# Four-layer network on one core: the first feed-forward layer's weights are loaded during the attention before it

## The chip, the cores and the metric

The kernel is one program on one core of a Trainium2 chip. It has five engines with a queue of their own (TensorE or PE, VectorE or DVE, ScalarE or ACT, GpSimd or POOL, SyncE or SP); SP issues nearly all DMAs. The metric is the device time of one execution in microseconds (us); lower is better. The time before the change is the median of three runs, 3949.11 us (3946.87 to 3950.89).

## What is computed

Four layers run one after the other on 2048 tokens of width 256 (2 sequences of 1024). Each layer normalises its input once and adds the outputs of an attention part and of a feed-forward part, both computed from that same normalised input. The first layer is the one that matters here:

```python
xn = _layernorm(x, axis=-1)
x = x + _L0_attn_ref(xn, w_q, w_kv, w_dense) + _L0_ffn_ref(xn, SU_ug, SU_dp, Wscale_ug, Wscale_dp, W_up, W_gate, W_down)

# attention: 16 heads of 128 in 4 groups, causal softmax
q, k, v = xn @ w_q, xn @ w_k, xn @ w_v
out = (softmax(mask(q @ k.T * scale)) @ v) @ w_dense

# feed-forward, 1024 wide; fwht is a normalised Walsh-Hadamard transform
x = fwht(x * SU_ug) / SCALE
x_up = x @ W_up.T * (Wscale_ug[:INTER] * SCALE)
x_gate = x @ W_gate.T * (Wscale_ug[INTER:] * SCALE)
x = jax.nn.silu(x_gate) * x_up
x = fwht(x * SU_dp) / SCALE
x = x @ W_down.T * (Wscale_dp * SCALE)
```

The kernel applies the transforms to the weights instead of the tokens: before the first token is multiplied, W_up, W_gate and W_down are multiplied by a Hadamard matrix and split into a high and a low part.

## The kernel before

A `Stage` is a scope: it allocates buffers and semaphores and gives them back at its end. Inside it, an `nc.Block` holds one instruction stream for each engine. All engines meet at a barrier at the end of a block, so nothing of the next block, its DMAs included, is issued before the last engine of this one is done. Within a block only semaphores order the engines; each engine takes its own instructions strictly in the order written, and so does SP with its DMAs.

`program` (L2735) runs the first layer as a normalisation, a split of the tokens into high and low parts, then `l0_attn` (L209), a block that clears semaphores, and `l0_ffn` (L550).

`l0_heads` (L274) loops over 16 heads. Each head has 16 blocks of 128 queries (`U`), and for these 20 software-pipelined steps s. In step s, PE makes the scores of block s (L355), transposes the probabilities of block s-2 (L369), multiplies the context of block s-4 by the dense weights (`dense`, L391) and weighs the values of block s-3 (L382). ACT in step s copies the context of block s-4 (L521), copies transposed probabilities (L514) and computes the exponentials of block s (L528). In step 4 (`SPLIT_AT`), between the copies and the exponential, ACT rounds the next head's query weights: `split_weights(h+1)` (L490 to L492), which waits for their load.

SP's stream in this block is short. It loads `wq` and `wd` of head 0 (L318, L319) and then loops over the other heads: the load of `wq` for head h waits for `wlo_ready` (L322, the previous head's query weights are used up), the load of `wd` for head h waits for `dense_done` of the previous head (L324). `wq` has one buffer.

`l0_ffn` begins with a small stage of its own, `l0w`: SP issues nine loads (L581 to L589: the Hadamard matrix `had`, `raw` for W_up and W_gate, `rawd` for W_down, and five small columns). DVE waits for all nine (`loaded`, L626) and negates `had` (L627); PE waits for that and multiplies `raw` and `rawd` by `had` (L600, L606); ACT and DVE split the products; DVE then does the rest of the transform of W_down (L645 to L654). Only after this block does the loop over tokens begin (L661 on).

```python
                def split_weights(h):
                    act.wait_ge(wq_loaded, h * 16 + 16)
                    wait(act, q_made, h * NJ)
                    act.activation(wq_hi[:, :, :], wq[:, :, :], ACT.Copy).then_inc(whi_ready, 1)
```

Of the kernel before, what the change touches and what calls it, by code (L numbers as in the profile page):

```python
# [16 lines left out]
P = 128  # L17
# [3 lines left out]
DC = D // P  # L21
# [6 lines left out]
class Stage:  # L28
# [5 lines left out]
    def __init__(self, nc, name):  # L34
        self.nc, self.name, self.ctx = nc, name, ExitStack()
# [35 lines left out]
def rows(w):  # L71

    return w.rearrange("(c p) n -> p c n", p=P)
# [134 lines left out]

def l0_attn(nc, k, a):  # L209
    with Stage(nc, "l0a") as st:  # L210
        KT = st.sb("KT", [P, L0_GROUPS, T])
        V = st.sb("V", [P, TT, L0_GROUPS * L0_HD])
        l0_kv(nc, k, a, KT, V)
        l0_heads(nc, k, a, KT, V)

# [57 lines left out]

def l0_heads(nc, k, a, KT, V):  # L274

# [7 lines left out]
    with Stage(nc, "l0h") as st:  # L283
# [22 lines left out]
        ctxT_ready, probs_scaled, vg_ready, copies = st.sem("ctxT_ready"), st.sem("probs_scaled"), st.sem("vg_ready"), st.sem("copies")  # L306
        dense_done, added = st.sem("dense_done"), st.sem("added")

        SPLIT_AT = 4
# [4 lines left out]
        with nc.Block() as block:  # L314

            @block.sync
            def _(sp):
                sp.dma_start(wq[:, :, :], rows(a["L0_attn_w_q"])[:, :, 0:P]).then_inc(wq_loaded, 16)  # L318
                sp.dma_start(wd[:, :], a["L0_attn_w_dense"][0:P, :]).then_inc(wd_loaded, 16)  # L319
                with sp.Fori(1, L0_HEADS) as h:  # L320
                    sp.wait_ge(wlo_ready, h)
                    sp.dma_start(wq[:, :, :], rows(a["L0_attn_w_q"])[:, :, ds(h * P, P)]).then_inc(wq_loaded, 16)  # L322
                    sp.wait_ge(dense_done, h * U)
                    sp.dma_start(wd[:, :], a["L0_attn_w_dense"][ds(h * P, P), :]).then_inc(wd_loaded, 16)  # L324

                sp.wait_ge(wlo_ready, L0_HEADS)
                sp.dma_start(wq[:, :, :], rows(a["L0_attn_w_q"])[:, :, 0:P]).then_inc(wq_loaded, 16)

            @block.tensor
# [219 lines left out]

def l0_ffn(nc, k, a):  # L550


    with Stage(nc, "l0f") as st:
# [3 lines left out]
        wd_hi, wd_lo = st.sb("wd_hi", [P, L0_FC, D], F32R), st.sb("wd_lo", [P, L0_FC, D], F32R)  # L557
        su = st.sb("su", [P, DC])
        sd = st.sb("sd", [P, L0_FC])
        su_n = st.sb("su_n", [P, DC])  # L560
        sd_n = st.sb("sd_n", [P, L0_FC])
        s_up = st.sb("s_up", [P, L0_FC])
        s_gate = st.sb("s_gate", [P, L0_FC])
        s_down = st.sb("s_down", [P, DC])
        with Stage(nc, "l0w") as s2:
            had = s2.sb("had", [P, 2, P])
            raw = s2.sb("raw", [P, 2, DC, L0_INTER])
            rawd = s2.sb("rawd", [P, L0_FC, D])
            bf0 = s2.sb("bf0", [P, L0_FC, D])
# [3 lines left out]
            acc = [s2.ps(f"acc{i}") for i in range(8)]  # L573
            loaded, made, kept, had_ready, flown = s2.sem("loaded"), s2.sem("made"), s2.sem("kept"), s2.sem("had_ready"), s2.sem("flown")
            NL = 9

            with nc.Block() as block:

                @block.sync
                def _(sp):  # L580
                    sp.dma_start(had[:, 0, :], a["c_had"]).then_inc(loaded, 16)  # L581
                    sp.dma_start(su[:, :], a["L0_ffn_SU_ug_cols"]).then_inc(loaded, 16)
                    sp.dma_start(raw[:, 0, :, :], rows(a["L0_ffn_W_upT"])).then_inc(loaded, 16)
                    sp.dma_start(raw[:, 1, :, :], rows(a["L0_ffn_W_gateT"])).then_inc(loaded, 16)
                    sp.dma_start(rawd[:, :, :], rows(a["L0_ffn_W_downT"])).then_inc(loaded, 16)
                    sp.dma_start(sd[:, :], a["L0_ffn_SU_dp_cols"]).then_inc(loaded, 16)
                    sp.dma_start(s_up[:, :], a["L0_ffn_Wscale_ug_cols"][:, 0:L0_FC]).then_inc(loaded, 16)
                    sp.dma_start(s_gate[:, :], a["L0_ffn_Wscale_ug_cols"][:, L0_FC:2 * L0_FC]).then_inc(loaded, 16)
                    sp.dma_start(s_down[:, :], a["L0_ffn_Wscale_dp_cols"]).then_inc(loaded, 16)  # L589

# [34 lines left out]
                def _(dve):  # L625
                    dve.wait_ge(loaded, 16 * NL)  # L626
                    dve.tensor_scalar(had[:, 1, :], had[:, 0, :], -1.0, None, ALU.mult).then_inc(had_ready, 1)  # L627
# [2103 lines left out]
SPLIT_LAYERS = (0, 1)  # L2731
LAYERS = [(l0_attn, l0_ffn), (l1_attn, l1_ffn), (l2_attn, l2_ffn), (l3_attn, l3_ffn)]


def program(nc, a):  # L2735


    with ExitStack() as ctx:
# [12 lines left out]
        for i, (attn, ffn) in enumerate(LAYERS):  # L2751
            norm_stage(nc, k, f"n{i}", k.XT, k.XN)
            with Stage(nc, f"x{i}") as sx:
                if i in SPLIT_LAYERS:
                    k.XH, k.XL = sx.sb("XH", [P, DC, T], F32R), sx.sb("XL", [P, DC, T], F32R)
                    split_stage(nc, f"s{i}", k.XN, k.XH, k.XL)
                attn(nc, k, a)
                clear_semaphores(nc)
                ffn(nc, k, a)
                clear_semaphores(nc)  # L2760

# [48 lines left out]
```

## Time and profile before

| | |
|---|---|
| median of three runs | 3949.11 us (3946.87 to 3950.89) |
| span of the profiled execution | 3953.8 us |
| PE busy | 3518.6 us, 89% of the span |
| DVE, ACT, POOL busy | 60%, 39%, 35% of the span |
| DMA engines busy | about 15% of 16 engines' span |
| first layer's attention (`l0_heads`) | from 99 to 1043 us of the span |
| first layer's weight loads and transforms (`l0w`) | from 1043 to 1089 us |

For the profiled execution the profile gives its span and no time beside it. The span runs from the first to the last instruction and is 4.7 us, or 0.1%, longer than the median of the timed runs. In the trace, PEclk is the TensorE clock that was granted in a stretch, as a share of full speed: 1.00 is 2.4 GHz and 0.50 is 1.2 GHz. "Idle before <-X" in brackets is the time for which the engine waited before the instruction and what ended the wait. SPq stands for SP's queue of DMA issues; an issue is short, and the data land later ("us to landing" counts from the issue).

### The profile page before, as it was taken

The numbers are of one execution on the slowest core, as the hardware profiler recorded it, in microseconds if no ns is written. First come the engines' busy times: TensorE is split into PE (matmuls) and PEld (weight loads), VectorE is DVE, ScalarE is ACT, GpSimd is POOL, SyncE is SP. The second block draws the span as 40 slices with busy tenths as digits, with TensorE's granted clock in tenths as the row PEclk, the third lists the DMA queues.
The fourth block names the chain that finished last, engine by engine and source line by source line (L and its number), as shares of the span: only waits on it lengthen the run. The fifth ranks groups of instructions, "written<-read, shape, count | busy, mean of one in ns | idle before, by whom it ended". The sixth has DMA issues, their size and how long they took to land. (4 is left out here: it accounts for less than half of the span.)

```text
span 3953.8 us, 65993 instructions
## 1 busy us (share of the span) xinstructions
PE 3518.6 (89%) x21608; PEld 2645.3 (67%) x21608; DVE 2363.0 (60%) x4783; ACT 1546.2 (39%) x2820; POOL 1385.1 (35%) x1085
## 2 busy tenths in 40 slices
PE   6899999999796999999995779998699988999576
PEld 4777777777574888888872445554388847886354
DVE  3555555655423566666654879885477756776454
ACT  2444444444333444444432236664333333333121
POOL 1333333332133666666652200000133352335144
PEclk8999999999898999999997879999799998999755
DMA  0000000000001000000000412221233304331144
GB/s 33 7 5 3 5 5 3 5 5 5 33 0 43 13 18 17 17 17 17 17 5 22 171 65 82 80 83 39 65 93 103 105 10 107 98 96 48 60 108 96
DMA packets 115990, 178.66 MB, mean 45 GB/s; under 512 B 22288, under 2 KB 65040, under 8 KB 115600
## 3 DMA queue, kind: packets, MB, share of 16 engines
q1 hardware_dynamic: 109776, 169.38, 13.7%
q0 software_dynamic: 6144, 8.39, 1.3%
q8 instruction: 38, 0.62, 0.1%
q14 instruction: 32, 0.26, 0.0%
HBM read 151.51 MB, written 25.95 MB: 45 GB/s over the span
## 5 line engine op out<-in xcount | busy, mean ns | idle before, releaser
L424 POOL TENSOR_TENSOR l0h_probs<-l0h_probs,l0h_inv 128x128 f32<-128x128 f32 (+7 forms) x256 | 292.7, 1146 | 585.4 <-DVE l0h_inv L459 585.4
L1775 DVE TENSOR_REDUCE l2h_half<-l2h_s 128x1 f32<-128x512 f32 x512 | 337.3, 685 | 48.0 <-PE l2h_s L1677 47.0
L355 PE MATMUL l0h_sc<-l0a_KT,l0h_QT 128*128 x768 | 296.7, 499 | 29.8 <-ACT l0h_probs L528 28.3
L1762 ACT ACTIVATE l2h_PT<-l2h_s 128x1024 f32<-128x1024 f32 x256 | 248.3, 1022 | 162.6 <-PE l2h_s L1687 162.5
L382 PE MATMUL l0h_cx<-l0h_PT,l0h_VG 128*128 128x128 f32 x2304 | 300.7, 276 | 0.0
L528 ACT ACTIVATE l0h_probs<-l0h_sc,l0h_negtop 128x128 f32<-128x128 f32 (+7 forms) x256 | 189.6, 741 | 245.0 <-DVE l0h_negtop L454 244.6
L382 PEld LDWEIGHTS l0h_cx<-l0h_PT,l0h_VG 128*128 128x128 f32 x2304 | 278.0, 192 | 1.1
L159 POOL TENSOR_TENSOR XN<-XN,n_rstd 128x512 f32<-128x512 f32 x32 | 39.8, 1266 | 595.8 <-DVE n_rstd L140 595.8
L1677 PE MATMUL l2h_s<-l2h_K,l2h_Q 128*128 128x512 f32 x512 | 218.5, 466 | 23.2 <-DMA l2h_K<-l_split 21.0
L452 DVE TENSOR_REDUCE l0h_top<-l0h_sc 128x1 f32<-128x128 f32 (+7 forms) x256 | 193.9, 758 | 8.8
L355 PEld LDWEIGHTS l0h_sc<-l0a_KT,l0h_QT 128*128 128x128 f32 x768 | 125.7, 192 | 106.3 <-issue 63.6
L391 PE MATMUL l0h_outp<-l0h_ctxT,l0h_wd 128*128 128x128 f32 x1024 | 163.8, 283 | 24.8 <-ACT l0h_ctxT L521 11.7
L369 PEld LDWEIGHTS l0h_tp<-ident,l0h_probs 128*128 128x128 f32 x1152 | 138.6, 141 | 64.1 <-issue 39.5
L1677 PEld LDWEIGHTS l2h_s<-l2h_K,l2h_Q 128*128 128x128 f32 x512 | 99.2, 195 | 113.4 <-DVE l2h_half L1775 74.7
L369 PE MATMUL l0h_tp<-ident,l0h_probs 128*128 128x128 f32 x1152 | 168.7, 273 | 0.0
L470 DVE COPY l0h_PT<-l0h_tp 128x256 f32<-128x256 f32 (+2 forms) x192 | 98.6, 514 | 114.2 <-PE l0h_tp L369 112.4
L2189 POOL TENSOR_TENSOR l3p_w_lo<-l3p_w,l3p_w_hi 128x1024 fp32r<-128x1024 f32 x34 | 80.1, 2356 | 241.1 <-ACT l3p_w_hi L2145 241.1
L391 PEld LDWEIGHTS l0h_outp<-l0h_ctxT,l0h_wd 128*128 128x128 f32 x1024 | 134.2, 191 | 44.7 <-ACT l0h_ctxT L521 31.2
L514 ACT ACTIVATE l0h_PT<-l0h_tp 128x512 f32<-128x512 f32 (+1 forms) x192 | 100.8, 525 | 159.8 <-PE l0h_tp L369 159.3
L2221 DVE TENSOR_TENSOR_SCAN l3p_table<-l3p_decb,l3p_eye 128x512 f32<-128x512 f32 x128 | 149.6, 1210 | 22.8 <-DMA l3p_blk<-c_l_block 17.3
L1687 PE MATMUL l2h_s<-l2h_Q,l2h_K 128*128 128x512 f32 x512 | 161.7, 399 | 0.0
L2179 POOL TENSOR_TENSOR l3a_Y<-l3p_skip,l3p_sz 128x512 f32 (+1 forms) x64 | 81.6, 1276 | 208.9 <-DVE l3p_skip L2212 208.9
(408 smaller groups left out, 8954.9 us busy)
## 6 DMA issues: line engine op xcount, KB each, us to landing
l3p_decb<-l_decays SPq DMA_DIRECT2D x128, 256.0 KB, 4.2
l3p_w<-L_w SPq DMA_DIRECT2D x34, 512.0 KB, 3.7
l2h_Q<-l_split SPq DMA_DIRECT2D x64, 256.0 KB
l2h_K<-l_split SPq DMA_DIRECT2D x64, 256.0 KB
l3p_prow<-l_decays SPq DMA_DIRECT2D x128, 128.0 KB, 2.9
l_split<-l2q_hi SPq DMA_DIRECT2D x16, 512.0 KB, 4.1
l_split<-l2q_lo SPq DMA_DIRECT2D x16, 512.0 KB, 3.8
mx_wgu<-L_ffn_w_gate_up SPq DMA_DIRECT2D x32, 256.0 KB
```

The source lines that it names most:

```text
L355: mm = pe.matmul(sc[u % 2][:, lo:lo + n], QT[:, u * P:(u + 1) * P], KT[:, ds(g, 1), b * S + lo:b * S + lo + n], start=True, stop=True)
L369: mm = pe.transpose(tp[n % 2][:, (kb - q) * P:(kb - q + 1) * P], probs[:, u % 4, kb * P:(kb + 1) * P], k.ident[:, :])
L382: mm = pe.matmul(cx[:, 0:P], VG[:, b * NQ + kb, :], PT[:, u % 2, kb, :], start=(kb == 0), stop=(kb == t))
L391: mm = pe.matmul(outp[:, c * P:(c + 1) * P], wd[:, c * P:(c + 1) * P], ctxT[:, u % 2, :], start=True, stop=True)
L424: pool.tensor_tensor(p, p, inv[:, u % 4:u % 4 + 1].to_broadcast([P, keys(u)]), ALU.mult).then_inc(probs_scaled, 1)
L452: dve.reduce_max(top[:, u % 2:u % 2 + 1], sc[u % 2][:, 0:keys(u)], AX_X).then_inc(top_ready, 1)
L528: act.activation(probs[:, u % 4, 0:keys(u)], sc[u % 2][:, 0:keys(u)], ACT.Exp, bias=negtop[:, u % 2:u % 2 + 1], scale=L0_SCALE, accum_out= ...
L1677: pe.matmul(bank(slot_of(i))[:, :], Q1[:, b, t * P:(t + 1) * P], K1[:, b, z * BANK:(z + 1) * BANK], start=True, stop=True).then_inc(s1_mad ...
L1687: mm = pe.matmul(s2[kb % 2][:, z * BANK:(z + 1) * BANK], K2[:, b, kb * P:(kb + 1) * P], Q2[:, b, z * BANK:(z + 1) * BANK], start=True, sto ...
L1762: act.activation(PT[:, b, kb, :], s2[kb % 2][:, :], ACT.Exp, scale=L2_SCALE).then_inc(exped, 1)
L1775: dve.reduce_max(half[:, b, t, z:z + 1], bank(slot_of(i))[:, :], AX_X).then_inc(s1_read, 1)
L2221: dve.tensor_tensor_scan(table[:, i, :], decb[:, o, i, :], eye4[:, :], 0.0, ALU.mult, ALU.add).then_inc(tables, 1)
```

## The change

The nine buffers that the feed-forward part's loads fill move into a class `L0Weights`, in a stage `l0r` that is open over both the attention and the feed-forward part, so that they lie beside the attention's buffers instead of in their place. The nine loads move from the feed-forward part's first block into SP's stream in `l0_heads`: behind the loads of head 0's weights and a new wait for the first `dense_done`, and ahead of the loop over the other heads. At the end of its stream SP waits until all nine have landed. The stage `l0w` has no SP stream any more, and DVE's wait for `loaded` is gone. All other instructions are the same.

```diff
@@ -206,12 +206,35 @@
 L0_SCALE = L0_HD ** -0.5
-def l0_attn(nc, k, a):
+class L0Weights:
+
+
+    def __init__(self, st):
+        self.had = st.sb("had", [P, 2, P])
+        self.raw = st.sb("raw", [P, 2, DC, L0_INTER])
+        self.rawd = st.sb("rawd", [P, L0_FC, D])
+        self.su = st.sb("su", [P, DC])
+        self.sd = st.sb("sd", [P, L0_FC])
+        self.s_up = st.sb("s_up", [P, L0_FC])
+        self.s_gate = st.sb("s_gate", [P, L0_FC])
+        self.s_down = st.sb("s_down", [P, DC])
+
+
+def l0_layer(nc, k, a):
+    with Stage(nc, "l0r") as st:
+        raws = L0Weights(st)
+        l0_attn(nc, k, a, raws)
+        clear_semaphores(nc)
+        l0_ffn(nc, k, a, raws)
+        clear_semaphores(nc)
+
+
+def l0_attn(nc, k, a, raws):
     with Stage(nc, "l0a") as st:
         KT = st.sb("KT", [P, L0_GROUPS, T])
         V = st.sb("V", [P, TT, L0_GROUPS * L0_HD])
         l0_kv(nc, k, a, KT, V)
-        l0_heads(nc, k, a, KT, V)
+        l0_heads(nc, k, a, KT, V, raws)
 def l0_kv(nc, k, a, KT, V):
@@ -305,6 +328,8 @@
         turned, pt_act, pt_dve, pv_done = st.sem("turned"), st.sem("pt_act"), st.sem("pt_dve"), st.sem("pv_done")
         ctxT_ready, probs_scaled, vg_ready, copies = st.sem("ctxT_ready"), st.sem("probs_scaled"), st.sem("vg_ready"), st.sem("copies")
         dense_done, added = st.sem("dense_done"), st.sem("added")
+        raw_loaded = st.sem("raw_loaded")
+        NL = 9
         SPLIT_AT = 4
@@ -317,6 +342,16 @@
             def _(sp):
                 sp.dma_start(wq[:, :, :], rows(a["L0_attn_w_q"])[:, :, 0:P]).then_inc(wq_loaded, 16)
                 sp.dma_start(wd[:, :], a["L0_attn_w_dense"][0:P, :]).then_inc(wd_loaded, 16)
+                sp.wait_ge(dense_done, 1)
+                sp.dma_start(raws.had[:, 0, :], a["c_had"]).then_inc(raw_loaded, 16)
+                sp.dma_start(raws.su[:, :], a["L0_ffn_SU_ug_cols"]).then_inc(raw_loaded, 16)
+                sp.dma_start(raws.raw[:, 0, :, :], rows(a["L0_ffn_W_upT"])).then_inc(raw_loaded, 16)
+                sp.dma_start(raws.raw[:, 1, :, :], rows(a["L0_ffn_W_gateT"])).then_inc(raw_loaded, 16)
+                sp.dma_start(raws.rawd[:, :, :], rows(a["L0_ffn_W_downT"])).then_inc(raw_loaded, 16)
+                sp.dma_start(raws.sd[:, :], a["L0_ffn_SU_dp_cols"]).then_inc(raw_loaded, 16)
+                sp.dma_start(raws.s_up[:, :], a["L0_ffn_Wscale_ug_cols"][:, 0:L0_FC]).then_inc(raw_loaded, 16)
+                sp.dma_start(raws.s_gate[:, :], a["L0_ffn_Wscale_ug_cols"][:, L0_FC:2 * L0_FC]).then_inc(raw_loaded, 16)
+                sp.dma_start(raws.s_down[:, :], a["L0_ffn_Wscale_dp_cols"]).then_inc(raw_loaded, 16)
                 with sp.Fori(1, L0_HEADS) as h:
                     sp.wait_ge(wlo_ready, h)
                     sp.dma_start(wq[:, :, :], rows(a["L0_attn_w_q"])[:, :, ds(h * P, P)]).then_inc(wq_loaded, 16)
@@ -325,6 +360,7 @@
                 sp.wait_ge(wlo_ready, L0_HEADS)
                 sp.dma_start(wq[:, :, :], rows(a["L0_attn_w_q"])[:, :, 0:P]).then_inc(wq_loaded, 16)
+                sp.wait_ge(raw_loaded, 16 * NL)
             @block.tensor
             def _(pe):
@@ -547,7 +583,7 @@
 L0_FC = L0_INTER // P
-def l0_ffn(nc, k, a):
+def l0_ffn(nc, k, a, raws):
     with Stage(nc, "l0f") as st:
@@ -555,38 +591,19 @@
         wu_hi, wu_lo = st.sb("wu_hi", [P, DC, L0_INTER], F32R), st.sb("wu_lo", [P, DC, L0_INTER], F32R)
         wg_hi, wg_lo = st.sb("wg_hi", [P, DC, L0_INTER], F32R), st.sb("wg_lo", [P, DC, L0_INTER], F32R)
         wd_hi, wd_lo = st.sb("wd_hi", [P, L0_FC, D], F32R), st.sb("wd_lo", [P, L0_FC, D], F32R)
-        su = st.sb("su", [P, DC])
-        sd = st.sb("sd", [P, L0_FC])
         su_n = st.sb("su_n", [P, DC])
         sd_n = st.sb("sd_n", [P, L0_FC])
-        s_up = st.sb("s_up", [P, L0_FC])
-        s_gate = st.sb("s_gate", [P, L0_FC])
-        s_down = st.sb("s_down", [P, DC])
+        had, raw, rawd, su, sd = raws.had, raws.raw, raws.rawd, raws.su, raws.sd
+        s_up, s_gate, s_down = raws.s_up, raws.s_gate, raws.s_down
         with Stage(nc, "l0w") as s2:
-            had = s2.sb("had", [P, 2, P])
-            raw = s2.sb("raw", [P, 2, DC, L0_INTER])
-            rawd = s2.sb("rawd", [P, L0_FC, D])
             bf0 = s2.sb("bf0", [P, L0_FC, D])
             bf1 = s2.sb("bf1", [P, L0_FC, D])
             wdn = s2.sb("wdn", [P, L0_FC, D])
             low, wd_ready = s2.sem("low"), s2.sem("wd_ready")
             acc = [s2.ps(f"acc{i}") for i in range(8)]
-            loaded, made, kept, had_ready, flown = s2.sem("loaded"), s2.sem("made"), s2.sem("kept"), s2.sem("had_ready"), s2.sem("flown")
-            NL = 9
+            made, kept, had_ready, flown = s2.sem("made"), s2.sem("kept"), s2.sem("had_ready"), s2.sem("flown")
             with nc.Block() as block:
-
-                @block.sync
-                def _(sp):
-                    sp.dma_start(had[:, 0, :], a["c_had"]).then_inc(loaded, 16)
...
-                    sp.dma_start(s_down[:, :], a["L0_ffn_Wscale_dp_cols"]).then_inc(loaded, 16)
                 @block.tensor
                 def _(pe):
@@ -623,7 +640,6 @@
                 @block.vector
                 def _(dve):
-                    dve.wait_ge(loaded, 16 * NL)
                     dve.tensor_scalar(had[:, 1, :], had[:, 0, :], -1.0, None, ALU.mult).then_inc(had_ready, 1)
                     dve.tensor_scalar(su_n[:, :], su[:, :], D ** -0.5, None, ALU.mult).then_inc(had_ready, 1)
                     dve.tensor_scalar(sd_n[:, :], sd[:, :], L0_INTER ** -0.5, None, ALU.mult).then_inc(had_ready, 1)
@@ -2729,7 +2745,7 @@
 SPLIT_LAYERS = (0, 1)
-LAYERS = [(l0_attn, l0_ffn), (l1_attn, l1_ffn), (l2_attn, l2_ffn), (l3_attn, l3_ffn)]
+LAYERS = [(None, None), (l1_attn, l1_ffn), (l2_attn, l2_ffn), (l3_attn, l3_ffn)]
 def program(nc, a):
@@ -2754,10 +2770,13 @@
                 if i in SPLIT_LAYERS:
                     k.XH, k.XL = sx.sb("XH", [P, DC, T], F32R), sx.sb("XL", [P, DC, T], F32R)
                     split_stage(nc, f"s{i}", k.XN, k.XH, k.XL)
-                attn(nc, k, a)
-                clear_semaphores(nc)
-                ffn(nc, k, a)
-                clear_semaphores(nc)
+                if i == 0:
+                    l0_layer(nc, k, a)
+                else:
+                    attn(nc, k, a)
+                    clear_semaphores(nc)
+                    ffn(nc, k, a)
+                    clear_semaphores(nc)
```

**Where the instructions stand.** The first place is SP, from the loads of head 0's weights on. Names beginning with l0h are the attention's buffers, l0w and l0f the feed-forward part's, l0r the new stage's. Before, the loop's load of `wq` (L322) stood two rows behind head 0's, and the nine loads stood in the next block, of which this shows only the start of the list:

```order
L318 DMA l0h_wq<-L_attn_w_q 128x2x128
L319 DMA l0h_wd<-L_attn_w_dense 128x256
L320 UNCONDITIONAL_BRANCH
L322 ISA [waits l0h_wlo_ready]
L322 DMA l0h_wq<-L_attn_w_q 128x2x128
L323 REGISTER_ALU
L324 ISA [waits l0h_dense_done]
L324 DMA l0h_wd<-L_attn_w_dense 128x256
L320 REGISTER_ALU
```

Now, from the row behind head 0's two loads on:

```order
L346 DMA l0r_had<-c_had 128x128 [waits l0h_dense_done]
L347 DMA l0r_su<-L_ffn_SU_ug_cols 128x2
L348 DMA l0r_raw<-L_ffn_W_upT 128x2x1024
L349 DMA l0r_raw<-L_ffn_W_gateT 128x2x1024
L350 DMA l0r_rawd<-L_ffn_W_downT 128x8x256
L351 DMA l0r_sd<-L_ffn_SU_dp_cols 128x8
L352 DMA l0r_s_up<-L_ffn_Wscale_ug_cols 128x8
L353 DMA l0r_s_gate<-L_ffn_Wscale_ug_cols 128x8
L354 DMA l0r_s_down<-L_ffn_Wscale_dp_cols 128x2
L355 UNCONDITIONAL_BRANCH
L357 ISA [waits l0h_wlo_ready]
L357 DMA l0h_wq<-L_attn_w_q 128x2x128
```

The nine loads and a wait for `dense_done` now stand between the load of `wd` for head 0 and the load of `wq` for head 1.

The second place is DVE, at the start of the feed-forward part's weight stage. Before:

```order
L624 UNCONDITIONAL_BRANCH [waits barrier_Pool_Activation_PE_DVE_SP_release]
L627 TENSOR_SCALAR l0w_had<-l0w_had 128x128 [waits l0w_loaded]
L628 TENSOR_SCALAR l0f_su_n<-l0f_su 128x2
L629 TENSOR_SCALAR l0f_sd_n<-l0f_sd 128x8
L636 SCALAR_TENSOR_TENSOR l0f_wu_lo<-l0w_acc,l0f_su_n,l0f_wu_hi 128x512 [waits l0w_had_ready,l0w_kept]
```

Now:

```order
L641 UNCONDITIONAL_BRANCH [waits barrier_Pool_Activation_PE_DVE_SP_release]
L643 TENSOR_SCALAR l0r_had<-l0r_had 128x128
L644 TENSOR_SCALAR l0f_su_n<-l0r_su 128x2
L645 TENSOR_SCALAR l0f_sd_n<-l0r_sd 128x8
L652 SCALAR_TENSOR_TENSOR l0f_wu_lo<-l0w_acc,l0f_su_n,l0f_wu_hi 128x512 [waits l0w_had_ready,l0w_kept]
```

The wait for `l0w_loaded` is gone; the order is the same.

The third place is ACT, in step 4 of a head, in the changed kernel; before, the same rows stand there, with L528 as L492 and L564 as L528:

```order
L550 ACTIVATE l0h_PT<-l0h_tp 128x384 [waits l0h_pv_done,l0h_turned]
L526 ISA
L80 REGISTER_ALU [waits l0h_wq_loaded]
L528 ACTIVATE l0h_wq_hi<-l0h_wq 128x256 [waits l0h_q_made]
L560 REGISTER_ALU
L564 ACTIVATE l0h_probs,l0h_total<-l0h_sc,l0h_negtop 128x640 [waits l0h_turned,l0h_negtop_ready]
```

Nothing moved on ACT: its wait for `wq_loaded` stands ahead of the exponential of the fifth block (L564).

## Rows read from the trace of the kernel before

**Rows 1.** The page's first line.

```profile
span 3953.8 us, 65993 instructions
```

**Rows 2.** Stretches: length, busy us (instructions) of each engine, PEclk, DMA share, GB/s.

```profile
99.00:1043.00 944.00, 884.32 (x5656) 707.45 (x5656) 527.50 (x1473) 421.49 (x1061) 312.41 (x281) 0.99 0.02 5
1043.00:1088.70 45.70, 19.45 (x40) 8.31 (x40) 18.06 (x29) 10.19 (x17) 0.00 (x0) 0.76 0.21 71
```

**Rows 3.** Timeline at the border of attention and feed-forward: start us, us, engine.

```profile
1041.28 0.71 PE L391 MATMUL l0h_outp<-l0h_ctxT,l0h_wd 128*128 128x128 f32 x4 [0.37 <-ACT l0h_ctxT L521]
1042.02 0.42 DVE L475 TENSOR_TENSOR XT<-XT,l0h_outp 128x256 f32<-128x256 f32 x1 [2.44 <-PE l0h_outp L391]
1043.24 0.34 SPq L581 DMA_DIRECT2D l0w_had<-c_had  x1
...
1045.10 0.47 SPq L585 DMA_DIRECT2D l0w_rawd<-L_ffn_W_downT  x1
1045.61 3.25 SPq L586 DMA_DIRECT2D l0f_sd<-L_ffn_SU_dp_cols  x1
...
1049.91 0.43 SPq L589 DMA_DIRECT2D l0f_s_down<-L_ffn_Wscale_dp_cols  x1
1055.87 0.23 DVE L627 TENSOR_SCALAR l0w_had<-l0w_had 128x128 f32<-128x128 f32 x1 [13.42 <-DMA l0f_s_down<-L_ffn_Wscale_dp_cols]
...
1056.15 16.02 PE L600 MATMUL l0w_acc<-l0w_raw,l0w_had 128*128 128x512 f32 x32 [14.16 <-DVE l0w_had L627]
```

**Rows 4.** DMA issues from 1040 to 1060 us: KB each, us to landing.

```profile
l0w_raw<-L_ffn_W_upT SPq DMA_DIRECT2D x1, 1024.0 KB, 5.4
...
l0w_rawd<-L_ffn_W_downT SPq DMA_DIRECT2D x1, 1024.0 KB, 9.5
...
l0f_sd<-L_ffn_SU_dp_cols SPq DMA_DIRECT2D x1, 4.0 KB, 9.2
...
l0f_s_down<-L_ffn_Wscale_dp_cols SPq DMA_DIRECT2D x1, 1.0 KB, 5.9
```

**Rows 5.** Stretches about the weight transforms, columns as in rows 2.

```profile
1042.00:1044.00 2.00, 0.00 (x0) 0.00 (x0) 0.42 (x1) 0.00 (x0) 0.00 (x0) 1.00 0.00 0
...
1046.00:1048.00 2.00, 0.00 (x0) 0.00 (x0) 0.00 (x0) 0.00 (x0) 0.00 (x0) 0.65 1.01 389
...
1056.00:1060.00 4.00, 3.85 (x5) 1.78 (x6) 0.24 (x3) 0.00 (x0) 0.00 (x0) 0.50 0.00 0
...
1062.00:1076.00 14.00, 13.60 (x32) 5.70 (x30) 5.26 (x7) 6.87 (x11) 0.00 (x0) 1.00 0.00 0
```

**Rows 6.** Timeline of head 0 about its step 4, columns as in rows 3.

```profile
103.14 0.39 SPq L322 DMA_DIRECT2D l0h_wq<-L_attn_w_q  x1
...
119.60 0.68 PE L391 MATMUL l0h_outp<-l0h_ctxT,l0h_wd 128*128 128x128 f32 x4
...
120.04 0.41 ACT L492 ACTIVATE l0h_wq_hi<-l0h_wq 128x256 fp32r<-128x256 f32 x1
...
120.84 0.79 ACT L528 ACTIVATE l0h_probs<-l0h_sc,l0h_negtop 128x640 f32<-128x640 f32 x1 [0.39 <-DVE l0h_negtop L454]
...
122.29 0.61 PE L391 MATMUL l0h_outp<-l0h_ctxT,l0h_wd 128*128 128x128 f32 x4
```

**Rows 7.** Timeline at the end of head 0, columns as in rows 3.

```profile
169.11 0.71 PE L391 MATMUL l0h_outp<-l0h_ctxT,l0h_wd 128*128 128x128 f32 x4 [0.37 <-ACT l0h_ctxT L521]
...
169.99 0.35 SPq L324 DMA_DIRECT2D l0h_wd<-L_attn_w_dense  x1
```

**Rows 8.** DMA issues from 99 to 121 us, columns as in rows 4.

```profile
l0h_wq<-L_attn_w_q SPq DMA_DIRECT2D x2, 128.0 KB, 2.2
```

**Rows 9.** Stretches early in the attention, columns as in rows 2.

```profile
101.00:102.00 1.00, 0.00 (x0) 0.00 (x0) 0.00 (x0) 0.26 (x1) 0.00 (x0) 0.55 0.64 179
...
103.00:107.00 4.00, 3.99 (x9) 3.14 (x10) 0.00 (x0) 0.60 (x1) 1.93 (x2) 0.50 0.11 33
...
121.00:131.00 10.00, 10.00 (x66) 7.86 (x65) 7.41 (x19) 4.93 (x12) 5.08 (x4) 1.00 0.01 2
```

More of the change, by code:

```diff
@@ L271, in _, with l0_heads @@
                     dve.tensor_copy(target(n), acc[n % 8][:, :]).then_inc(kept_dve, 1)
-def l0_heads(nc, k, a, KT, V):
+def l0_heads(nc, k, a, KT, V, raws):
     U = B * NQ
@@ L573, in l0_ffn @@
             acc = [s2.ps(f"acc{i}") for i in range(8)]
-            loaded, made, kept, had_ready, flown = s2.sem("loaded"), s2.sem("made"), s2.sem("kept"), s2.sem("had_ready"), s2.sem("flown")
-            NL = 9
+            made, kept, had_ready, flown = s2.sem("made"), s2.sem("kept"), s2.sem("had_ready"), s2.sem("flown")
             with nc.Block() as block:
-                @block.sync
-                def _(sp):
-                    sp.dma_start(had[:, 0, :], a["c_had"]).then_inc(loaded, 16)
[L582 to L588, printed above, removed]
-                    sp.dma_start(s_down[:, :], a["L0_ffn_Wscale_dp_cols"]).then_inc(loaded, 16)
                 @block.tensor
```

## The prediction

> **What bounds the kernel now.** I read the stretches by stage first. The attention of the first layer takes 944 us with PE busy for 884 of them; the stretch behind it, in which the feed-forward weights are loaded and transformed, takes 45.7 us with PE busy for 19.5 [rows 2]. So PE bounds the attention, and the stretch behind it is a chain of waits. The timeline shows the chain. The last matmul of the attention ends at 1041.99 (1041.28 + 0.71), the last DVE instruction at 1042.44; SP issues the first of nine loads at 1043.24; DVE negates the Hadamard matrix only at 1055.87, released by the ninth load; PE begins at 1056.15 [rows 3]. Look at the bracket of the DVE row: 13.42 us idle, ended by a DMA. No engine has work in these 12.6 us, so they lie wholly on the path. The landing times tell why it lasts that long: three loads of 1 MB keep all 16 DMA engines busy (share 1.01, 389 GB/s [rows 5]), and a 4 KB load issued behind them lands 9.2 us after its issue [rows 4].
>
> The second place to read is where the loads go. In head 0 the load of `wq` for head 1 is issued at 103.14 and used by ACT at 120.04: it has 17 us and needs 2.2 [rows 6, 8]. In the changed order it stands behind a wait for the first `dense_done` and behind the nine loads, and ACT's wait for it stands ahead of an exponential that everything else in the head hangs on. That is where I look for the price.
>
> **Part 1, the loads leave the feed-forward part: a gain of 12.6 us.** DVE's first instruction now waits only for the barrier. The barrier let SP go at 1043.24 [rows 3]; I let DVE start at the same time, 12.6 us earlier. All loads have landed some 900 us before. Bounds: 12.3 (a barrier that frees DVE 0.3 later) to 12.7.
>
> **Part 2, the clock in the transforms: a gain of 2.2 us.** PE's granted clock is still 1.00 from 1042 to 1044, is falling from 1046 to 1048 (mean 0.65), and is at 0.50 when the transforms begin: from 1056 to 1060 PE needs 3.85 us for 5 matmul records, later 13.60 us for 32, or 0.43 each [rows 5]. Now PE is idle only from 1041.99 to about 1043.5, a time through which the clock stayed at 1.00 before. At full clock the 32 records take 13.6 us plus some 0.2 for the last to end, against 16.02 [rows 3, 5], so 2.2 us less. Everything up to the end of the transforms follows PE here. Bounds: 0 (the clock falls all the same) to 2.4.
>
> **Part 3, ACT waits in head 0: a loss of 13.0 us.** First, when SP goes on. At the end of head 0 the dense matmuls begin at 169.11 and SP's issue that waits for them comes at 169.99, 0.88 later [rows 7]. The first dense matmuls begin at 119.60 [rows 6], so SP issues its first moved load at about 120.5. The nine issues took 7.1 us before (1043.24 to 1049.91 + 0.43, one of them 3.25 us long [rows 3]), so `wq` is issued at about 127.6. The ninth load landed 12.6 us after the first issue (1049.91 + 5.9 = 1055.8 [rows 3, 4]), now at 133.1. `wq` is 128 KB behind it, 0.3 us at 389 GB/s, and lands at 133.4. ACT's rounding starts there in place of 120.04, 13.4 us late. Behind it on ACT is the exponential of block 4; it used to wait 0.39 us for DVE [rows 6] and will not any more, so it comes 13.0 us late. Behind that on ACT is the copy of context 1, for which PE's dense matmuls of 122.29 wait [rows 6]; PE, DVE and POOL have only what is already released, about 2 us of it. From 121 to 131 PE was busy for 10.00 of 10 us [rows 9], so there is no slack in which the head could catch up.
>
> Bounds: the lower is a `wq` that lands 2.2 us after its issue [rows 8], at 129.8, whatever is before it: a loss of 9.4. The upper is 14, if the transfers are a tenth slower than they were with every engine idle. I take the value behind the queue, because the nearest row is the 4 KB load that needed 9.2 us behind 3 MB [rows 4]. The page "DMA: Bandwidth & Descriptors" of the Trainium skill, section "Queues, rings and completion order", says that completion is "not FIFO per issuing engine". Taken by itself for `wq`, that would make this part 9.4 and the time 3945.9 us. The small load's 9.2 us in this trace speaks for the same page's other sentence, that each DMA engine takes up its ring in order.
>
> **Part 4, the clock in head 0: a loss of 2.2 us.** PE stands still from about 122.3 to 135. A pause of this length took the clock to 0.50 at the border [rows 5], and a shorter one at 101 us did too (mean 0.55 [rows 9]). On its return PE worked at 0.50 for at least 4 us, busy for 3.99 of them [rows 9]. Where PE is the bound, half of such a time is lost: 2.0 for 4 us, 2.5 for 5, and I take 2.2. Bounds: 0 (PE has no full work then) to 2.75 (5.5 us).
>
> **At nothing.** SP's wait at the end of the block costs nothing while the loads land 900 us earlier; if they did not, the barrier would wait for them. The load of `wd` for head 1 still waits for the end of head 0. The buffers' new addresses and the missing SP stream cost nothing that the trace shows. The layers behind are unchanged.
>
> **Sum.** -12.6 - 2.2 + 13.0 + 2.2 = +0.4 us. The profiled execution spans 3953.8 us [rows 1], 4.7 more than the median; I add the difference to the median, 3949.11 + 0.4 = 3949.5 us. The load has not left the path, it has moved from one border to one head. With the bounds of all parts together the difference runs from -5.7 (-12.7 - 2.4 + 9.4 + 0) to +4.5 (-12.3 + 0 + 14 + 2.75, rounded).
>
> **The rivals.** About 0.2% of the time, 7.9 us, is what a measurement of this kernel can tell from no change.
>
> *A, `wq` overtakes the large loads.* For it: 128 KB is little, and nothing orders the loads but the queue. Against it: the 9.2 us of 4 KB [rows 4]. Then part 3 is 9.4 and the time 3945.9 us. Chance 0.09.
>
> *B, the clock falls at the border all the same.* For it: the row of 101 us shows a fall within a short pause [rows 9]. Against it: 1.00 from 1042 to 1044 [rows 5]. Part 2 is 0, the time 3951.7 us. Chance 0.09.
>
> *C, faster: the heads take up the stall.* In the attention PE is idle for 60 of 944 us [rows 2]. If the engines behind ACT had work in store, or the stall used up waits that come anyway, parts 3 and 4 would vanish and 3934.3 us would be left. Against it: PE is at 10.00 of 10 us where the stall falls [rows 9], and each block needs its exponential. Chance 0.07.
>
> *D, slower: PE stays at the low clock in head 0.* After the stall PE works in a chain with ACT and DVE; if its pauses keep the clock at 0.50, half of each microsecond of its work is lost. It decides from about 19 us at the low clock: 9.5 in place of 2.2 makes the sum +7.7. If it lasts for the rest of head 0, some 49 us of PE work (120 to 169) become 98, and the time is 3996 us. Against it: after 103 us the clock was back at 1.00 by 121 [rows 9]. Chance 0.07.
>
> *E, the change does not do what it says*, in that something else still holds DVE at the border. The barrier's own time is in the 1043.24; nothing else stands ahead of L643. It would leave +15 us; I hold it within D's 0.07.
>
> **How the numbers follow.** The forecast has 0.68, A and B 0.09 each, C and D 0.07 each. A and B lie within 7.9 us, so: faster 0.07, same 0.86, slower 0.07. The range is 3943 to 3955 us: the sum of all bounds gives 3943.4 to 3953.6, and the three runs before spread over 4 us. C and D are left out.
>
> **What would show it.** In the changed kernel DVE negates the matrix about 0.8 us behind the attention's last DVE instruction; the transforms run at clock 1.00 from the start; ACT's second rounding in head 0 has an idle time of about 13 us ended by the load of `wq`; PE has a hole of about 12 us behind its scores of block 5, and the clock is at 0.50 for 4 to 5 us behind it. Head 1 begins about 15 us later than before. I am wrong if that hole is not there or is much shorter, if `wq` lands before `rawd`, or if any other stage differs by more than a microsecond or two.

## The result, and the profile after

| | before | after |
|---|---|---|
| median | 3950.76 us (3944.20 to 3958.32, 20 runs) | 3959.11 us (3949.59 to 3962.67, 20 runs) |
| span of the profiled execution | 3953.8 us | 3957.9 us |

The changed kernel is slower: ratio 1.0018, 95% interval 1.0011 to 1.0024, or 7.1 us (4.3 to 9.5) on 3951; the two medians lie 8.35 us apart, and this text goes by the ratio. The forecast was 3949.5 us and no change, within 3943 to 3955. It was built on 3949.11 us, the median of three runs; twenty give 3950.76, so 1.65 of the 9.6 us between forecast and measurement are the base.

Two words for what follows: the border is the time from the attention's last addition (DVE) to the negation of the Hadamard matrix (DVE), and the kv projection is the block ahead of the heads in which PE makes keys and values (`l0_kv`). The moved buffers are eight, not nine: two of the nine loads fill `raw`.

Head 0 of the changed kernel, timeline (start us, us, engine):

```profile
123.75 0.94 PE L427 MATMUL l0h_outp<-l0h_ctxT,l0h_wd 128*128 128x128 f32 x4
...
124.72 0.34 SPq L346 DMA_DIRECT2D l0r_had<-c_had  x1
...
127.08 2.81 SPq L351 DMA_DIRECT2D l0r_sd<-L_ffn_SU_dp_cols  x1
...
131.94 0.40 SPq L357 DMA_DIRECT2D l0h_wq<-L_attn_w_q  x1
137.76 0.42 ACT L528 ACTIVATE l0h_wq_hi<-l0h_wq 128x256 fp32r<-128x256 f32 x1 [13.27 <-DMA l0h_wq<-L_attn_w_q]
138.09 0.78 ACT L564 ACTIVATE l0h_probs<-l0h_sc,l0h_negtop 128x640 f32<-128x640 f32 x1
...
138.85 0.27 ACT L557 ACTIVATE l0h_ctxT<-l0h_cx 128x128 f32<-128x128 f32 x1
...
139.17 1.22 PE L427 MATMUL l0h_outp<-l0h_ctxT,l0h_wd 128*128 128x128 f32 x4 [12.31 <-ACT l0h_ctxT L557]
```

The wait that was foretold is there: ACT's second rounding sits idle for 13.27 us, ended by the load of `wq`, and PE has a hole of 12.31 us behind it. Set against [rows 6, 7]: SP's first moved load comes 0.97 us after the dense matmuls begin (0.88 in the forecast), `wq` is issued 7.2 us after that (7.1 in the forecast), and the rounding follows 13.0 us after the first issue (12.9). The landing times, columns as in [rows 4]:

```profile
l0r_rawd<-L_ffn_W_downT SPq DMA_DIRECT2D x1, 1024.0 KB, 9.9
l0h_wq<-L_attn_w_q SPq DMA_DIRECT2D x1, 128.0 KB, 5.7
...
l0r_sd<-L_ffn_SU_dp_cols SPq DMA_DIRECT2D x1, 4.0 KB, 9.6
```

`wq`, last in the queue, lands at 131.94 + 5.7 = 137.6, and `rawd`, which was issued at 126.57, at 126.57 + 9.9 = 136.5: `wq` did not overtake the large loads. The 128 KB that took 2.2 us alone [rows 8] took 5.7.

The border, timeline; before it was [rows 3]:

```profile
1062.66 0.71 PE L427 MATMUL l0h_outp<-l0h_ctxT,l0h_wd 128*128 128x128 f32 x4 [0.37 <-ACT l0h_ctxT L557]
1063.41 0.42 DVE L511 TENSOR_TENSOR XT<-XT,l0h_outp 128x256 f32<-128x256 f32 x1 [2.44 <-PE l0h_outp L427]
1064.68 0.23 DVE L643 TENSOR_SCALAR l0r_had<-l0r_had 128x128 f32<-128x128 f32 x1 [0.85 <-PEq L60]
```

From the last addition to the negation there are 1.27 us where there were 13.84. The first 32 records of the transforms, PE's timeline by itself:

```profile
1064.96 14.00 PE L617 MATMUL l0w_acc<-l0r_raw,l0r_had 128*128 128x512 f32 x32 [1.59 <-DVE l0r_had L643]
```

14.00 us in place of 16.02. The clock, stretches with columns as in [rows 2]:

```profile
139.00:145.00 6.00, 5.83 (x17) 4.08 (x18) 2.98 (x8) 1.39 (x4) 3.40 (x3) 0.51 0.00 0
145.00:151.00 6.00, 6.00 (x45) 5.00 (x44) 4.46 (x10) 3.11 (x6) 1.68 (x1) 1.00 0.00 0
...
1064.00:1066.00 2.00, 1.04 (x3) 0.56 (x4) 0.47 (x3) 0.00 (x0) 0.00 (x0) 1.00 0.01 4
```

PE is at full clock at the border (1064 to 1066). In head 0 it is at 0.51 for the 6 us behind the hole and at 1.00 after it. So each foretold step is there, in about its size. Something else is in the trace, and it begins before SP has issued anything new: in the kv projection, 50 us ahead of the moved loads. PE there fills one bank of results with 6 matmuls after another, and DVE copies every second bank, so that 12 matmuls lie between two copies. The timeline of before, then of after:

```profile
74.05 0.69 DVE L271 COPY l0a_KT<-l0kv_acc 128x512 f32<-128x512 f32 x1 [2.03 <-PE l0kv_acc L199]
76.77 0.69 DVE L271 COPY l0a_KT<-l0kv_acc 128x512 f32<-128x512 f32 x1 [2.03 <-PE l0kv_acc L199]
```

```profile
73.58 0.69 DVE L294 COPY l0a_KT<-l0kv_acc 128x512 f32<-128x512 f32 x1 [2.11 <-PE l0kv_acc L199]
76.38 0.69 DVE L294 COPY l0a_KT<-l0kv_acc 128x512 f32<-128x512 f32 x1 [2.11 <-PE l0kv_acc L199]
```

Twelve matmuls take 2.72 us before and 2.80 after, 0.227 and 0.233 us each. Those are matmuls of the keys. For the values, which follow, the view by tile gives the duration of one (ns, min/median/max), before and after:

```profile
L199 PE MATMUL l0kv_acc<-l0kv_w_hi,x_XH x32: 389/389/389, 76.6 to 97.6; 128*128 128x512 f32 x32
```

```profile
L199 PE MATMUL l0kv_acc<-l0kv_w_hi,x_XH x32: 391/397/400, 79.0 to 100.8; 128*128 128x512 f32 x32
```

They are the same instructions on the same data; of the two operands that PE reads, the tokens (`XH`, `XL`) lie where they lay, and the weights (`l0kv_w_hi`, `l0kv_w_lo`) have moved.

I divided each trace at fixed instructions. "To layer 1" runs from the load of the kv weights to layer 1's first load; "loop" is from the first gate matmul to the last addition. Head 15 and layer 1's normalisation have no column, so the columns do not add up to "to layer 1". The rows below after are kernels of the next section. Times in us:

| kernel | kv projection | head 0 | heads 1 to 14 | border | weight stage | loop | to layer 1 |
|---|---|---|---|---|---|---|---|
| before | 55.13 | 59.11 | 814.04 | 13.84 | 32.86 | 139.88 | 1219.78 |
| after | 57.09 | 75.90 | 815.49 | 1.27 | 30.82 | 141.29 | 1225.67 |
| e5_top | 55.26 | 73.57 | 814.41 | 1.27 | 30.82 | 139.77 | 1220.20 |
| e7_stall_alone | 55.33 | 73.70 | 814.82 | 13.77 | 33.82 | 138.72 | 1234.20 |
| e3_wq_first | 56.77 | 60.45 | 815.38 | 1.27 | 32.42 | 141.34 | 1211.33 |
| e6_top_wq_first | 55.34 | 59.12 | 814.30 | 1.27 | 30.81 | 138.75 | 1203.70 |
| e8_wq_between | 55.43 | 60.95 | 814.57 | 1.27 | 32.51 | 140.14 | 1209.70 |

After is 5.9 us behind before at layer 1, while its columns add up to 7.0. The other 1.1 us came back in layer 1's normalisation, between the loop's last addition and layer 1's first load: there PE's clock fell 18.6 us behind the last addition in the kernel before and 23.5 us behind it in the changed one. These stretches begin 18.6 us behind it, before and after:

```profile
1248.00:1252.80 4.80, 2.38 (x3) 0.33 (x1) 3.05 (x2) 0.69 (x1) 2.48 (x2) 0.50 0.00 0
```

```profile
1256.20:1261.00 4.80, 1.23 (x3) 0.19 (x1) 4.18 (x2) 0.69 (x1) 2.48 (x2) 1.00 0.00 0
```

The early fall is in before, e4, e5 and e8 to e11, the late one in after, e1, e2, e3, e6 and e7, so it goes with no one edit; it moves the time to layer 1 by 0.8 to 1.3 us. What follows layer 1's first load is unchanged code and takes 2689.7 us before and 2686.7 after; over all kernels here it took 2679 to 2690, with nothing that goes with the edit. That scatter is why the two spans (4.1 us apart) do not say the same as the medians.

### The profile page after: what moved, and what is told of

Same layout as the page of the kernel before. It is cut to its first block and busy times, and to the rows that moved or that the text cites. A ratio compares the mean times of both kernels' runs of the same rounds, so it can differ in the third digit from the quotient of the medians.

```text
span 3957.9 us, 65994 instructions
## 1 busy us (share of the span) xinstructions
PE 3521.8 (89%) x21608; PEld 2645.4 (67%) x21608; DVE 2363.8 (60%) x4783; ACT 1548.0 (39%) x2820; POOL 1374.1 (35%) x1085
## 5 line engine op out<-in xcount | busy, mean ns | idle before, releaser
L564 ACT ACTIVATE l0h_probs<-l0h_sc,l0h_negtop 128x128 f32<-128x128 f32 (+7 forms) x256 | 189.8, 741 | 244.1 <-DVE l0h_negtop L490 243.7
```

What stands on the lines that cost most here:

```text
L564: act.activation(probs[:, u % 4, 0:keys(u)], sc[u % 2][:, 0:keys(u)], ACT.Exp, bias=negtop[:, u % 2:u % 2 + 1], scale=L0_SCALE, accum_out= ...
```

## The experiments

There are two theories. A: the surplus over the forecast comes from the addresses to which the eight buffers, allocated first, push all others, and the sum of the forecast is right. B: it comes from the loads, the longer scope or a worse stall.

**The changed kernel, padded.** In e1, 32 unused bytes per partition lie behind the moved buffers:

```diff
         self.s_down = st.sb("s_down", [P, DC])
+        self.pad = st.sb("pad", [P, 8])
```

> The changed kernel with one spare column block of 32 bytes per partition behind the moved buffers, so that every buffer of the first layer starts 32 bytes later. Theory of the addresses (a 512-column matmul is slower when its two operands start in different 32-byte halves of a 64-byte line): the spacing of the key and value projection's matmuls falls from 0.234 us back to 0.227, its stage from 57.1 to 55.5 us, the gate and up projections' spacing too, and the time is 3 to 6 us below the changed kernel's, so about 0 to 4 us above the kernel before. Rival (the slower spacing is the chip's or the run's): spacing stays at 0.234 and the time at about 7 us above the kernel before.

Measured 3950.77 us, ratio 0.9999 (0.9991 to 1.0008). Thirty-two unused bytes took the loss away; layer 1 is reached 5.0 us sooner than in the changed kernel (1220.63), of which 1.1 is a clock that rose earlier in the loop, as in e6 below. Gate and up matmuls came to 0.229 us, but the kv projection stayed at 0.233: its expected fall to 0.227 did not come. So the 64-byte form of the theory is wrong, and which distance matters is taken up below.

**The kernel before, padded.** e2 is the reverse, 32 bytes ahead of the first layer's buffers and nothing else:

```diff
+                with Stage(nc, f"pad{i}") as sp_:
+                    if i == 0:
+                        sp_.sb("pad", [P, 8])
                     attn(nc, k, a)
```

> The kernel before with 32 bytes per partition ahead of the first layer's buffers, nothing else. Theory of the addresses: the spacing of the projections' matmuls rises from 0.227 to 0.234 us, the key and value stage takes 1.3 us more, the 16 heads together 1.5 to 2.6 more, gate and up 2.6 more, down no faster: 4 to 6 us above the kernel before. Rival: no difference in spacing or time.

Measured 3954.81 us, ratio 1.0012 (1.0002 to 1.0021). By tile:

```profile
L199 PE MATMUL l0kv_acc<-l0kv_w_hi,x_XH x32: 393/396/400, 78.9 to 100.6; 128*128 128x512 f32 x32
```

The matmuls are slow as in the changed kernel, with no load moved. "To layer 1" is 1225.33 us, 5.6 over before.

**The change with all old addresses.** In e5 the eight buffers are allocated from the other end of SBUF, the on-chip memory, and a gap stands where five of them, the small columns, stood in the feed-forward part:

```diff
-        self.had = st.sb("had", [P, 2, P])
+        def top(name, shape):
+            return st.ctx.enter_context(st.nc.sbuf_tensor(f"{st.name}_{name}", shape, F32, side="right"))
+        self.had = top("had", [P, 2, P])
...
         sd_n = st.sb("sd_n", [P, L0_FC])
+        st.sb("gap", [P, 40])
```

> The changed kernel with the eight moved buffers allocated from the other end of SBUF, and 160 bytes left unused in l0f where the columns stood, so that every buffer that PE reads in the first layer's kv projection, heads and token loop lies at the address it had before. If the changed kernel's surplus over the prediction is a matter of addresses (theory A): the kv projection takes about 55 to 56 us and its 512-column matmuls are 0.227 us apart as before, and what is left is the prediction's own sum, border -12.6, transforms -2.0, head 0 +15.2, together +0.6 us: ratio 1.0002, within 1.000 +- 0.001. If the surplus is a matter of something else in the change (theory B: the open stage, SP's stream, the loads' traffic), the spacing stays 0.233 us and the ratio stays at 1.0018.

Measured 3955.00 us against 3951.01, ratio 1.0005 (0.9996 to 1.0015). Tile and ACT's timeline:

```profile
L199 PE MATMUL l0kv_acc<-l0kv_w_hi,x_XH x32: 388/389/390, 76.6 to 97.7; 128*128 128x512 f32 x32
```

```profile
133.44 0.42 ACT L530 ACTIVATE l0h_wq_hi<-l0h_wq 128x256 fp32r<-128x256 f32 x1 [13.22 <-DMA l0h_wq<-L_attn_w_q]
```

The matmuls are back at 389 ns, the stall is there, and the table has +0.42 us at layer 1: kv 0.1, head 0 +14.5, heads +0.4, border -12.6, weight stage -2.0. The forecast's sum was +0.4. The time alone cannot confirm it: the interval is -1.6 to +5.9 us, which holds +0.4 and leaves out the changed kernel's 1.0018. But the stages leave theory B nothing: the loads, the scope and the stall are all still there, and layer 1 is reached 5.5 us sooner than in the changed kernel.

**The loss alone.** e7 is e5 with the nine loads issued once more at the border, and DVE's wait for them:

```diff
+                @block.sync
+                def _(sp):
+                    sp.dma_start(raws.had[:, 0, :], a["c_had"]).then_inc(loaded, 16)
...
+                    dve.wait_ge(loaded, 16 * 9)
                     dve.tensor_scalar(had[:, 1, :], had[:, 0, :], -1.0, None, ALU.mult).then_inc(had_ready, 1)
```

> e5 with the nine loads issued once more in the weight stage, and DVE's wait for them there: the first half of the change (loads in the attention, ahead of wq for head 1) with nothing gained at the border. The prediction's parts 3 and 4: head 0 is 15.2 us longer, the border 13 us as before, together +15.2 us, ratio 1.0038. If the rest of the attention took part of the stall back (the rival in which the heads absorb it), it would be under 1.003.

Measured 3963.87 us, ratio 1.0031 (1.0020 to 1.0042), 12 us (8 to 17); "to layer 1" +14.4. The wait at the border is as in [rows 3]:

```profile
1057.36 0.42 DVE L513 TENSOR_TENSOR XT<-XT,l0h_outp 128x256 f32<-128x256 f32 x1 [2.44 <-PE l0h_outp L429]
1058.58 0.34 SPq L613 DMA_DIRECT2D l0r_had<-c_had  x1
...
1071.13 0.23 DVE L660 TENSOR_SCALAR l0r_had<-l0r_had 128x128 f32<-128x128 f32 x1 [13.35 <-DMA l0r_s_down<-L_ffn_Wscale_dp_cols]
```

Heads 1 to 14 take none of the 14.6 us back (they are 0.8 longer): rival C is out.

**`wq` first.** The load of `wq` for head 1 goes ahead of the wait and the nine loads:

```diff
+                sp.wait_ge(wlo_ready, 1)
+                sp.dma_start(wq[:, :, :], rows(a["L0_attn_w_q"])[:, :, P:2 * P]).then_inc(wq_loaded, 16)
                 sp.wait_ge(dense_done, 1)
                 sp.dma_start(raws.had[:, 0, :], a["c_had"]).then_inc(raw_loaded, 16)
...
-                with sp.Fori(1, L0_HEADS) as h:
+                sp.wait_ge(dense_done, U)
+                sp.dma_start(wd[:, :], a["L0_attn_w_dense"][P:2 * P, :]).then_inc(wd_loaded, 16)
+                with sp.Fori(2, L0_HEADS) as h:
```

e3 has this edit at the changed kernel's addresses, e4 with e1's 32 bytes besides:

> The changed kernel with the query weights of head 1 loaded ahead of the wait and the nine loads, as in the kernel before. Theory of the stall (parts 3 and 4 of the prediction): ACT does not wait in head 0, PE has no hole; head 0 is 15 to 16 us shorter than in the changed kernel, and the time is 7 to 9 us below the kernel before (-14.8 from the border, some +5 from the addresses). Rival (the loads themselves, running beside the attention, cost the time): head 0 keeps a good part of its 16.7 us.

> Both edits together. Theory: 11 to 15 us below the kernel before (-14.8, and nothing for the addresses), ratio about 0.9967. If the addresses do not matter, the same as with the load order alone.

Measured 3942.30 us, ratio 0.9978 (0.9969 to 0.9988), and 3934.94 us, ratio 0.9954 (0.9941 to 0.9967). Head 0 is at 60.4 us in both. e4 came out better than expected: 18 us (13 to 23) by its ratio, where 11 to 15 were expected and its own trace is 10.2 us ahead of before's at layer 1 (1209.62 for 1219.78). That surplus is not explained. The transforms at the border gained little, here in e3:

```profile
1049.17 15.61 PE L621 MATMUL l0w_acc<-l0r_raw,l0r_had 128*128 128x512 f32 x32 [1.59 <-DVE l0r_had L647]
```

15.61 us against [rows 3]'s 16.02: the clock fell behind the pause here, and in e4, e8 and e10 too. PE was idle for the same 1.59 us in the changed kernel, and there the clock held, as it did in e1, e5, e6 and e9. That is rival B in some executions, for 1.6 us.

e6 is the same edit on e5, so with before's addresses:

> e5 with the load of wq for head 1 issued ahead of the wait for dense_done and of the nine loads (and wd for head 1 behind them). Theory A: the border gain of 12.6 us stands alone, the transforms' gain is 0.4 to 2, head 0 costs nothing: 12.6 to 14.6 us faster than before, ratio 0.9963 to 0.9968, spacing 0.227 us; the stall in head 0 is gone and the second rounding of wq follows its head's start by about 9 us. Theory B: as e3 (0.9978), 5 us slower than theory A.

Measured 3936.71 us, ratio 0.9961 (0.9947 to 0.9976). ACT and SP:

```profile
121.89 0.41 ACT L534 ACTIVATE l0h_wq_hi<-l0h_wq 128x256 fp32r<-128x256 f32 x1
122.00 0.34 SPq L350 DMA_DIRECT2D l0r_had<-c_had  x1
```

No idle time ahead of the rounding, head 0 is 59.12 us as before, and layer 1 is reached 16.1 us earlier. Border and weight stage give 14.6 of them. Another 1.1 is the loop, where PE's clock rose 3.2 us behind the first gate matmul in place of 5.7, which e7 has as well without this edit, and 1.1 is layer 1's normalisation with its late fall; neither belongs to the edit. The kv projection and heads 1 to 14 took 0.5 longer.

**Wait or queue?** e8 is e6 with `wq` behind the wait for `dense_done`, still ahead of the nine:

> e6 with the load of wq for head 1 behind the wait for dense_done, but ahead of the nine loads: the wait alone, without the queue. dense_done comes at about 120.5 us and the load takes 2.2 us: wq lands at 122.7, ACT's rounding comes 2.7 us late, of which the exponential's own wait of 0.4 hides a part, and the clock stays up: head 0 costs 2 to 3 us. With the border's 12.6 and the transforms' 0.4 to 2: 10 to 12.5 us faster than before, ratio 0.9968 to 0.9975. If the wait were most of the stall (and the nine loads little), head 0 would cost 9 us or more and the ratio would be above 0.999.

Measured 3939.32 us, ratio 0.9974 (0.9963 to 0.9985).

```profile
121.82 0.37 SPq L348 DMA_DIRECT2D l0h_wq<-L_attn_w_q  x1
...
122.23 0.47 SPq L349 DMA_DIRECT2D l0r_had<-c_had  x1
...
124.15 0.42 ACT L533 ACTIVATE l0h_wq_hi<-l0h_wq 128x256 fp32r<-128x256 f32 x1 [2.36 <-DMA l0h_wq<-L_attn_w_q]
```

The wait for `dense_done` alone costs ACT 2.36 us and head 0 1.8; the place behind nine loads costs the other 12.6 of 14.5.

**Which addresses?** Three kernels ask what the rule is. In e11, before's `XH` and `XL` move by 32 bytes along with everything behind them:

```diff
                 if i in SPLIT_LAYERS:
+                    if i == 0:
+                        sx.sb("pad", [P, 8])
```

> The kernel before with 32 unused bytes ahead of XH and XL of the first layer, so that XH, XL and all of the first layer's buffers behind them move by 32 bytes together. If it is the difference of the two operands' addresses that counts: 0.227 us for kv, gate and up, 0.230 for the query projection, down at 0.2333, and no change of the time (ratio 1.000). If it is each buffer's own remainder modulo 64 (32 fast, 0 slow): 0.2335 for all of them, as in e2, and the ratio 1.0012.

> e5 with 64 bytes left unused ahead of the attention's buffers alone: the kv weights and wq stand 64 bytes from the remainder of XH and XL modulo 128, and equal to it modulo 64. If only the remainder modulo 64 counts: kv projection 0.227 us apart. If the remainder modulo 128 counts: 0.229 to 0.233 for the kv projection, as in e1 and e4, where the difference was also 64; the token loop, which does not move, stays at 0.227 for gate and up.

> e6 with the unused bytes in l0f 192 in place of 160, so that hid_hi and hid_lo, the other operand of the down projection, move by 32 bytes and stand at the same remainder as wd_hi and wd_lo modulo 64 (and 128), which they did not even before. Theory A (two operands of a matmul that start at the same remainder modulo 64 make 512-column matmuls faster): the down projection's matmuls are 0.227 to 0.229 us apart in place of 0.2333, all other spacings as in e6, the token loop is about 1 us shorter (192 matmuls less 0.005 each), the time 13 to 16 us under before, ratio 0.996. If the rule is about something else than the two operands, the down projection stays at 0.2333.

Measured: e11 3949.12 us, ratio 1.0001 (0.9990 to 1.0011); e10 3956.75 us, one run; e9 3933.70 us, ratio 0.9965 (0.9952 to 0.9979). e10 is e5 with 64 bytes ahead of `KT`; e9 is e6 with 48 words of gap for 40. The value matmuls of the kv projection in e11 and in e10, then the down matmuls of before and of e9:

```profile
L199 PE MATMUL l0kv_acc<-l0kv_w_hi,x_XH x32: 389/389/389, 76.2 to 97.3; 128*128 128x512 f32 x32
```

```profile
L199 PE MATMUL l0kv_acc<-l0kv_w_hi,x_XH x32: 396/397/398, 77.5 to 99.2; 128*128 128x512 f32 x32
```

```profile
L681 PE MATMUL l0f_down<-l0f_hid_hi,l0f_wd_hi x64: 395/396/503, 1113.3 to 1227.6; 128*128 128x512 f32 x64
```

```profile
L704 PE MATMUL l0f_down<-l0f_hid_hi,l0f_wd_hi x64: 389/389/504, 1099.2 to 1212.4; 128*128 128x512 f32 x64
```

The table has, for each pair of operands, how far their start addresses are apart modulo 128 bytes (the shorter way round, worked out from the order of allocation with 32 bytes for each small column buffer, as e5's gap of 160 bytes has it for five), and behind the colon the mean distance of matmul starts in ns, from the traces at full clock:

| kernel | kv | query projection | gate and up | down |
|---|---|---|---|---|
| before, e5 | 0: 227 | 0: 230 | 0: 227 | 32: 233 |
| after | 32: 234 | 32: 233 | 32: 233 | 64: 229 |
| e1 | 64: 233 | 64: 230 | 64: 229 | 64: 229 |
| e2 | 32: 233 | 32: 233 | 32: 233 | 32: 233 |
| e10 | 64: 233 | 64: 233 | 0: 227 | 32: 233 |
| e11 | 0: 227 | 0: 230 | 0: 227 | 32: 233 |
| e9 | 0: 227 | 0: 230 | 0: 227 | 0: 228 |

e11 settles that it is the difference that counts and not the address: all moved together, and all stayed as they were. e9 sped up a projection that had been slow even before, by 1.2 us of the loop (137.53 for 138.75). Layer 1's first load did not come earlier for it: the clock of e9 fell early in layer 1's normalisation and that of e6 late, which took the 1.2 us back, so the gain shows in no time. A difference of 32 was slow in every row. At 64 it was 229 to 233 with nothing here that says which: e4, at e1's addresses, has 229 for the keys and 233 for the values. That stays open. So does the period: 64 bytes apart is not like 0, but no pair here stood 128 apart, so 128 is not told from a larger one.

## Why the prediction was wrong

*Part 1, the border, -12.6:* measured 13.84 - 1.27 = 12.57. *Part 2, the clock in the transforms, -2.2:* 2.0 in after and e5, 0.4 in e3, e4 and e8, where the clock fell; inside its bounds. *Parts 3 and 4, ACT's wait and the low clock behind it, +15.2:* 14.5 in e5, 14.6 in e7; the steps of the working (issue, queue, landing) were each met within 0.2 us. In e5 PE came back at 134.85 and had 3.9 us at 0.50, worth some 1.9 where 2.2 was forecast. The Trainium skill says in "DMA: Bandwidth & Descriptors", "Queues, rings and completion order", that completion is "not FIFO per issuing engine". That promises no order and forbids none; in this trace `wq` landed last, as the forecast had it. *Rivals:* A is out (5.7 us, behind `rawd`), C by e7, D since the clock is back at 1.00 by 145, E by the row of 1064.68. B came true in four of nine profiled executions with this pause, though not in the changed kernel's.

**The step that failed** is under "At nothing": "The buffers' new addresses and the missing SP stream cost nothing that the trace shows". With the sum of all other steps confirmed at +0.4 in e5, the addresses are the one thing in which the changed kernel differs from e5, and it reaches layer 1 5.5 us later (1225.67 less 1220.20): kv projection 1.8, head 0 2.3, the other heads 1.1, the loop 1.5 to its last addition, of which 0.3 is left at layer 1 since the clock in the normalisation fell late. By the ratios it is 1.0018 - 1.0005 = 0.0013, 5.1 us (0.6 to 9.7, an estimate from the two intervals), and e2, which has the addresses alone, gives 1.0012, 4.7 us (0.8 to 8.3).

The slower matmuls themselves make some 4.3 us, an estimate from the spacings: 192 of kv by 7 ns and 384 of the query projection by 3.4 ns are 1.3 each, 384 of gate and up by 6.6 ns are 2.5, and 192 of down are 4 ns faster, -0.8. That fits kv, the other heads and the loop, but not head 0, whose 24 query matmuls are worth 0.1. Head 0's share is the clock. The same 3 us of head 0, from 6 to 9 us behind DVE's first row maximum, before and after:

```profile
117.96:120.96 3.00, 3.00 (x17) 2.13 (x17) 2.44 (x8) 1.86 (x6) 1.24 (x2) 0.96 0.00 0
```

```profile
121.02:124.02 3.00, 3.00 (x10) 1.97 (x10) 1.71 (x6) 0.97 (x4) 1.25 (x2) 0.50 0.00 0
```

The low clock that follows the start of the heads lasts some 3 us longer in the changed kernel, worth about 1.5. Behind the stall PE had 5.7 us at 0.50 where e5 had 3.9, worth another 0.9. e1 to e4 have the longer low clock at the start as well (head 0 is 60.4 in e3 in place of 59.1), e5 to e9 and e11 don't. But neither does e10, whose kv and query matmuls are slow too and whose head 0 is no longer than e5's. So that the addresses lengthen the low clock is not shown; that part of head 0 may be chance. The range, 3943 to 3955, had no term for a cost of the addresses, and the text had said that a stage which differs by more than a microsecond or two would be the sign; the kv projection was that stage.

The trace of before held a hint: its down matmuls last 396 ns and its gate matmuls 389, with the same shape and type. The prediction used neither row.

## What to carry to other kernels

When buffers move, compare the start addresses of the two operands of each large matmul modulo 128 bytes. Unequal ones cost these 512-column matmuls 1 to 3%, and a pad of 32 bytes is a cheap trial (e1, e2). A load that moves earlier goes behind the small load that the next step waits for, never ahead of it: the order in SP's stream was worth 0.4% here (e3), twice what the change lost. And test an edit with all other buffers at their old addresses: only in e5, which has them there, could the forecast's sum of +0.4 be seen stage by stage.

## What was unexpected of the hardware

At full clock two 512-column matmuls of the kv, gate and up projections start 227 ns apart when weights and moving operand (the one that streams past the weights) start at the same remainder modulo 128, and 233 to 234 when 32 bytes apart. "TensorE: Matmul & The Clock Gate" of the Trainium skill, "Step-by-step: what each phase is for", says that loading the next weights "doesn't steal SBUF read bandwidth from the running matmul". The same instruction takes 389 ns or 396 ns here (before and e2), set apart by nothing but the two operands' relative start. So where the operands lie does matter to these matmuls; that it is the loading of the weights that takes the time was not tried, and the sentence may hold. The Trainium skill's page "SBUF — State Buffer", "Operand start alignment", speaks of legality and says that its runs "timed nothing". Also unexpected: after one and the same pause of 1.6 us at the border, PE's clock held in five profiled executions and fell in four, worth 1.6 us; no cause of it was found.
